# Turnings of x, context and maxima move into the ring of four working banks; their bank becomes a third score bank

## The reference, cut to what matters

```
x = x + layernorm(attention(layernorm(x)))     # 16 heads of 16, block-sparse: blocks of 64 tokens
x = x + layernorm(ffn(layernorm(x)))           # a dense "abel" branch, and 8 experts, the best 2 per token
```

## Time and profile before

| what | value |
|---|---|
| median of 3 runs (lowest to highest) | 1812.6 us (1811.93 to 1817.06) |
| profiled execution, its own time | 1810.62 us |
| its span, first to last instruction | 1808.8 us |
| PE busy | 1542.5 us, 85% |
| DVE busy | 1236.9 us, 68% |
| ACT busy | 897.1 us, 50% |
| POOL busy | 706.6 us, 39% |
| exponentials (L1006) | 768 of 600 ns |
| row maxima (L1168) | 1024 of 546 ns |
| mean granted TensorE clock | 0.956 of full speed |

### The profile page before, as it was taken

How to read it: one execution, slowest core, us unless ns; L and a number is a source line. 1 busy time by engine, 2 the same in 40 slices (tenths; PEclk the granted TensorE clock), 3 DMA queues, 4 the chain that set the end, 5 groups by cost and what they waited for, 6 DMA issues and landing times. The chain is left out here.

```text
span 1808.8 us, 33541 instructions
## 1 busy us (share of the span) xinstructions
PE 1542.5 (85%) x10381; PEld 1072.0 (59%) x10446; DVE 1236.9 (68%) x3681; ACT 897.1 (50%) x1785; POOL 706.6 (39%) x716
## 2 busy tenths in 40 slices
PE   3989999999998998999999888399999999999600
PEld 2645555555555554555555446288888888888500
DVE  6677787778778777877877744355556655565277
ACT  1146766676676667667666672133333333333234
POOL 0111323433343344244234334135444444445468
PEclk9899999999999999999999998699999999999855
DMA  3333235325424533543443226745656565655387
GB/s 100 117 118 98 86 118 171 116 98 173 140 98 154 166 109 106 170 141 112 137 159 117 90 91 199 236 100 102 147 103 146 103 152 105 141 117 112 36 308 251
DMA packets 184525, 241.49 MB, mean 134 GB/s; under 512 B 23560, under 2 KB 155024, under 8 KB 184272
## 3 DMA queue, kind: packets, MB, share of 16 engines
q1 hardware_dynamic: 157520, 203.58, 35.2%
q0 software_dynamic: 26880, 36.33, 12.1%
HBM read 133.40 MB, written 105.91 MB: 132 GB/s over the span
## 5 line engine op out<-in xcount | busy, mean ns | idle before, releaser
L1006 ACT ACTIVATE pexp<-scT 128x512 f32<-128x512 f32 x768 | 434.9, 600 | 275.5 <-PE scT L784 238.7
L1168 DVE TENSOR_REDUCE mx<-work 128x1 f32<-128x320 f32 (+2 forms) x1024 | 499.9, 546 | 70.4 <-PE work L757 70.4
L1679 POOL DMA_INDIRECT y_rows<-rows_add,row_of x144 | 226.5, 1573 | 294.6 <-DMA y_rows<-rows_add,row_of 207.9
L757 PE MATMUL work<-w 126*128 126x320 bf16 (+4 forms) x1280 | 274.9, 298 | 33.1 <-DVE mx L1168 29.6
L784 PE MATMUL scT<-w 128*128 128x192 bf16 (+3 forms) x1472 | 258.5, 270 | 26.0 <-ACT pexp L1006 20.6
L1711 PE MATMUL h_ps<-inT,w1c 128*128 128x256 f32 x1152 | 262.2, 381 | 2.6 <-DVE inT L1763 2.6
L1724 PE MATMUL o_ps<-w,hT 128*128 x1152 | 260.5, 380 | 0.0
L1654 ACT ACTIVATE rows_add<-rows_out,row_share 128x257 f32<-128x257 f32 x144 | 65.6, 503 | 355.5 <-DVE rows_out L1779 276.5
L1711 PEld LDWEIGHTS h_ps<-inT,w1c 128*128 128x128 f32 x1152 | 220.1, 191 | 33.2 <-issue 3.8
L1724 PEld LDWEIGHTS o_ps<-w,hT 128*128 128x128 f32 x1152 | 213.9, 191 | 25.7
L784 PEld LDWEIGHTS scT<-w 128*128 128x128 bf16 x1536 | 125.1, 97 | 162.3 <-ACT pexp L1006 110.4
(11 more groups left out here) (174 smaller groups left out, 2120.8 us busy)
## 6 DMA issues: line engine op xcount, KB each, us to landing
w<-split_spill SPq DMA_DIRECT2D x384, 128.0 KB, 2.9
split_spill<-split SPq DMA_DIRECT2D x64, 384.0 KB, 3.1
rows_in<-z_rows SPq DMA_DIRECT2D x72, 265.0 KB, 4.8
y_rows<-pre SPq DMA_DIRECT2D x16, 514.0 KB, 5.8
y<-y_rows SPq DMA_DIRECT2D x16, 514.0 KB, 6.7
x_rows<-x SPq DMA_DIRECT2D x16, 512.0 KB, 2.6
abel_rows<-pre SPq DMA_DIRECT2D x16, 512.0 KB, 3.5
abel_in<-abel_rows SPq DMA_DIRECT2D x16, 512.0 KB, 4.6
```

Source lines behind the costliest of these rows:

```text
L757: ins = nc.tensor.matmul(out[:, at:at + hi - lo], tile(qst[par][0:K_SCORE, h, :], t), kst[par][0:K_SCORE, h, lo:hi], start=True, stop=True)
L1006: nc.scalar.activation(pexp[:, (q * GROUP + n) % NPB, :], scT[n % 2][:, :], ACT.Exp, scale=DH ** -0.5).then_inc(s_exp, 1)
L1168: emptied(nc.vector.reduce_max(mx[:, c:c + 1], bank(s, "max", b, h, t)[:, 0:n], AX_X), s, "max", b, h, t)
L1679: pool.indirect_dma_start(kept.y_rows, bass.IndirectOffsetOnAxis(ap=row_of[n][:, r:r + 1], axis=0), rows_add[n % 2][:, r, :], None, comput ...
```

## The change

The bank `turn` becomes a third score bank: unit u uses bank u mod 3 and waits for the exponential of unit u-3. The two turnings of x (`xt`), the four of the context (`ctx`) and the two of the maxima (`turnmax`) become items of the ring, with its waits in place of the semaphores s_xt, s_xnT, s_mt, s_m2, s_turn and s_ctxn. In `order_of` each stands where TensorE issues it. On ScalarE the copies of x come after the first exponential of quads 8 and 10, not after the fourth, and the copy of the late maxima after the third exponential of quad 3. On VectorE the subtraction for the late maxima comes ahead of the last two maxima of quad 3, not behind them.

```diff
-        scT = [ps(f"scT{i}", [P, S]) for i in range(2)]
+        scT = [ps(f"scT{i}", [P, S]) for i in range(3)]
         pv = ps("pv", [P, S])
-        turn = ps("turn", [P, S])
...
             for m in range(4):
                 if here(s, 0):
                     seq.append(("project", m))
+                if here(s, 2) and m % 2:
+                    seq.append(("ctx", m // 2))
                 if here(s, 1):
                     maxima(s - 1, late("proj", m))
             if here(s, 3):
                 seq.extend(("z", k) for k in range(KC))
             for q in range(QUADS):
+                if q in TURN_XN and s + 1 < B:
+                    seq.append(("xt", TURN_XN.index(q)))
                 for n in range(GROUP):
                     if here(s, 0) and q < V_QUADS and n == 1:
                         seq.append(("value", q))
+                    if here(s, 2) and q < 2 and n == 2:
+                        seq.append(("ctx", q + 2))
+                    if here(s, 1) and q == LATE_TURN_AT and n == 2:
+                        seq.append(("turnmax", 1))
                     if here(s, 0):
                         maxima(s, fill(q, n))
                         if q == QUADS - 1:
+                            if n == 3:
+                                seq.append(("turnmax", 0))
                             maxima(s, late("end", n))
...
             def turn_xn(b, k):
-                if k == 0:
-                    wait(pe, s_ctxn, (b - 2) * NTOK)
-                    wait(pe, s_m2[1], b - 1)
-                wait(pe, s_xnT, b * KC + k)
+                out = use(b - 1, "xt", k)
...
             def turn_max(b, part):
                 reduced(pe, b, part)
-                if part:
-                    pe.wait_ge(s_m2[0], b + 1)
-                    wait(pe, s_ctxn, b * NTOK)
-                else:
-                    wait(pe, s_ctxn, (b - 1) * NTOK)
-                    pe.wait_ge(s_xnT, min(b + 2, B) * KC)
+                out = use(b + part, "turnmax", part)
...
-                wait(pe, s_exp, u - 1)
+                wait(pe, s_exp, u - 2)
                 for t, at, lo, hi in CHUNKS[c]:
-                    ins = nc.tensor.matmul(scT[n % 2][:, at:at + hi - lo],
+                    ins = nc.tensor.matmul(scT[u % 3][:, at:at + hi - lo],
...
             def turn_ctx(b, j):
                 if j == 0:
                     pe.wait_ge(s_ctxT, (b + 1) * NG)
-                    pe.wait_ge(s_xnT, min(b + 3, B) * KC)
-                    pe.wait_ge(s_m2[0], min(b + 2, B))
-                    pe.wait_ge(s_m2[1], b + 1)
-                wait(pe, s_ctxn, b * NTOK + j)
+                out = use(b + 2, "ctx", j)
...
# ScalarE, step
                         if attend:
                             exps(s - 1, q, n)
+                        if q in TURN_XN and n == 0 and s + 1 < B:
+                            evac_xnT(s + 1, TURN_XN.index(q))
+                        if attend and q == LATE_TURN_AT and n == 2:
+                            first_max(s - 1, 1)
...
-                    if attend and q == LATE_TURN_AT:
-                        first_max(s - 1, 1)
...
-                    if q in TURN_XN and (not isinstance(s, int) or s + 1 < B):
-                        evac_xnT(s + 1, TURN_XN.index(q))
...
# VectorE, step
                     if proj:
                         for n in range(1, GROUP):
+                            if n == 3 and attend and q == LATE_TURN_AT:
+                                second_max(s - 1, 1)
                             for h, t in fill(q, n):
                                 maximum(s, s, h, t)
...
-                    if attend and q == LATE_TURN_AT:
+                    if attend and not proj and q == LATE_TURN_AT:
                         second_max(s - 1, 1)
```

More of the change, by code:

```diff
@@ L437, in order_of @@
             if s < 0:
-                return [("series", n, i) for n in range(SERIES_FIRST) for i in range(NROT)]
+                return [("series", n, i) for n in range(SERIES_FIRST) for i in range(NROT)] \
+                    + [("xt", k) for k in range(KC)]
             seq = []
@@ L568, in put_maxima @@
             def put_maxima(par, b, part):
-                sp.wait_ge(s_m2[part], b + 1)
+                freed(sp, b + part, "turnmax", part)
                 heads = slice(EARLY, HEADS) if part else slice(0, EARLY)
@@ L713, in turn_xn @@
             def turn_xn(b, k):
-                if k == 0:
-                    wait(pe, s_ctxn, (b - 2) * NTOK)
-                    wait(pe, s_m2[1], b - 1)
-                wait(pe, s_xnT, b * KC + k)
+                out = use(b - 1, "xt", k)
                 for j in range(NTOK):
                     pe.wait_ge(s_xn, b * NTOK + j + 1)
-                    ins = nc.tensor.transpose(turn[:, j * P:(j + 1) * P], xn[:, j, k * P:(k + 1) * P],
+                    ins = nc.tensor.transpose(out[:, j * P:(j + 1) * P], xn[:, j, k * P:(k + 1) * P],
                                               ident_sb[:, :])
-                ins.then_inc(s_xt, 1)
+                filled(ins, b - 1, "xt", k)
             def project(b, m):
                 if m == 0:
-                    pe.wait_ge(s_xnT, (b + 1) * KC)
+                    for k in range(KC):
+                        freed(pe, b - 1, "xt", k)
                 col = (m % 2) * D + (m // 2) * P
@@ L765, in turn_max @@
                 reduced(pe, b, part)
-                if part:
-                    pe.wait_ge(s_m2[0], b + 1)
-                    wait(pe, s_ctxn, b * NTOK)
-                else:
-                    wait(pe, s_ctxn, (b - 1) * NTOK)
-                    pe.wait_ge(s_xnT, min(b + 2, B) * KC)
+                out = use(b + part, "turnmax", part)
                 plain(pe)
                 some = mx[:, NT * EARLY:] if part else mx[:, 0:NT * EARLY]
-                nc.tensor.transpose(turn[0:some.shape[1], 0:P], some, ident_sb[:, :]).then_inc(s_mt[part], 1)
+                filled(nc.tensor.transpose(out[0:some.shape[1], 0:P], some, ident_sb[:, :]),
+                       b + part, "turnmax", part)
             def score_unit(b, par, q, n):
@@ L964, in evac_xnT @@
             def evac_xnT(b, k):
-                act.wait_ge(s_xt, b * KC + k + 1)
-                nc.scalar.copy(xnT[:, k, :], turn[:, :]).then_inc(s_xnT, 1)
+                full(act, b - 1, "xt", k)
+                emptied(nc.scalar.copy(xnT[:, k, :], bank(b - 1, "xt", k)[:, :]), b - 1, "xt", k)
             def first_part(b, m):
@@ L980, in first_max @@
             def first_max(b, part):
-                act.wait_ge(s_mt[part], b + 1)
+                full(act, b + part, "turnmax", part)
                 wait(act, s_mrow[part], b * N_MAX * 16)
-                nc.scalar.copy(mrow[part][:, 0, :], turn[0:mrow[part].shape[0], 0:P]).then_inc(s_m1[part], 1)
+                nc.scalar.copy(mrow[part][:, 0, :], bank(b + part, "turnmax", part)[0:mrow[part].shape[0], 0:P])\
+                  .then_inc(s_m1[part], 1)
             def norm_x(b, p, j):
@@ L1010, in evac_ctx @@
                 act.wait_ge(s_pv, b * QUADS + (g + 1) * NCH)
-                if g == 0:
-                    wait(act, s_turn, b * NTOK)
+                if g == 0 and b > 0:
+                    for j in range(NTOK):
+                        full(act, b + 1, "ctx", j)
                 nc.scalar.copy(ctxT[:, g, :], pv[:, :]).then_inc(s_ctxT, 1)
@@ L1172, in second_max @@
                 dve.wait_ge(s_m1[part], b + 1)
-                nc.vector.tensor_tensor(mrow[part][:, 1, :], turn[0:mrow[part].shape[0], 0:P],
-                                        mrow[part][:, 0, :], ALU.subtract).then_inc(s_m2[part], 1)
+                emptied(nc.vector.tensor_tensor(mrow[part][:, 1, :],
+                                                bank(b + part, "turnmax", part)[0:mrow[part].shape[0], 0:P],
+                                                mrow[part][:, 0, :], ALU.subtract), b + part, "turnmax", part)
             def evac_z(s, b, k):
@@ L1184, in finish_a @@
             def finish_a(b, j):
-                dve.wait_ge(s_turn, b * NTOK + j + 1)
-                tv = turn[:, :].rearrange("p (h e) -> p h e", e=32)
+                full(dve, b + 2, "ctx", j)
+                tv = bank(b + 2, "ctx", j)[:, :].rearrange("p (h e) -> p h e", e=32)
                 nc.vector.reciprocal(rden[:, j % 2, :], tv[:, :, DH]).then_inc(s_rden, 1)
@@ L1193, in finish_a @@
                 inv = rden[:, j % 2, :].rearrange("p (h o) -> p h o", o=1).broadcast_to([P, HEADS, DH])
-                nc.vector.tensor_tensor(ctxn[:, j, :].rearrange("p (h d) -> p h d", d=DH),
-                                        tv[:, :, 0:DH], inv, ALU.mult).then_inc(s_ctxn, 1)
-                dve.wait_ge(s_ctxn, b * NTOK + j + 1)
+                emptied(nc.vector.tensor_tensor(ctxn[:, j, :].rearrange("p (h d) -> p h d", d=DH),
+                                                tv[:, :, 0:DH], inv, ALU.mult), b + 2, "ctx", j)
+                freed(dve, b + 2, "ctx", j)
```

12 lines of the change are left out of this document (3 added, 9 removed).

## The result

The changed kernel takes 1841.87 us (median of 4 runs, 1836.99 to 1844.55); the kernel before took 1814.05 us beside it (4 runs, 1811.93 to 1817.06). The ratio is 1.0153, with a 95% interval of [1.0127, 1.0179]. The forecast was 1832, its range 1815 to 1843: the sign and most of the ring's price came out as forecast, but about two fifths of the loss have a cause that the forecast did not hold, a falling clock.

What follows compares the result with a forecast made beforehand. TensorE was taken to bound the front, busy 755.51 of 820.22 us in full steps. Terms -2.1 - 2.0 + 4.9 + 13.7 + 5.0 = +19.5 us on the median 1812.6 gave 1832, range 1815 to 1843.

Steps and rivals of the forecast that it cites:

- The late maxima at quad 3: Quad 3's last maximum must wait for the subtraction that empties the turning: 1.05 us a step, x 13 = +13.7 us.
- rival C: Ring takes turnings with less loss: quad 3's last maximum loses 0.4 us, turnings of x nothing; 1818.5 us, chance 0.14.
- The project phase: Maximum waits for project 0, z 1 for project 3; most returns in quad 1, leaving 0.41 us x 12 = +4.9 us.
- Rival B: Project phase's delay is not taken back: TensorE stays 1.1 us late, not 0.41; 1840 us, chance 0.15.
- The turnings of x: At quads 8 and 10 each waits for a maximum, 0.18 and 0.24 us: 0.42 x 12 = +5.0 us.
- Quads 5 to 7 and 9: Score waits removed there are worth 0: TensorE then waits for the copied context or for VectorE at a maximum.
- Rival A: Score banks were the true limit: 20.6 us of waits come back and no added wait counts; 1792 us, chance 0.07.
- The third bank: In full steps it gains only at quad 11, where nothing but TensorE is late: -0.16 us x 13 = -2.1 us.
- The one-offs outside the full steps: Of 8.0 us of score waits outside the full steps, a quarter is saved: -2.0 us, bounds 0 and -8.0.

Runs made afterwards that it cites:

- e3: Kernel before, own turning bank kept; only the last maximum of quad 3 waits for the late maxima's subtraction, with copy and subtraction placed as changed: 1834.29 us, ratio 1.0118.
- e2: Changed kernel, but a score unit again waits for the exponential two units before, so the third bank gives no slack: 1849.07 us, ratio 1.0209.
- e4: Changed kernel with the two turnings of x at quads 9 and 11 instead of 8 and 10: 1829.83 us, ratio 1.0091.
- e8: Kernel before, own turning bank kept, with x turned at quads 9 and 11 and copied after the first exponential there: 1804.94 us, ratio 0.9956.
- e1: Changed kernel with the turning of the late maxima moved from quad 3 to the end of quad 4: 1836.10 us, ratio 1.0125.
- e7: Changed kernel with the late maxima turned ahead of quad 3's first maximum and subtracted first by VectorE: 1827.51 us, ratio 1.0077.
- e5: Changed kernel with late maxima turned sooner, x turned at quads 9 and 11, and the project phase's second maximum behind project 2: 1805.73 us, ratio 0.9969.

## Why the prediction was right in sign and 10 us short

By the profiled executions, +19.5 was forecast and +33.9 came, 14.4 more. Its terms, one by one:

- **The late maxima at quad 3: right.** 1.05 a step forecast; in step 6 TensorE is 0.43 late entering quad 3 and 1.47 late after it, 1.04 (lateness here is the start of the same matmul, counted from the step's start, against the kernel before); e3 gives the same 1.04 alone. It is the largest single term, with the releaser that was named, and rival C, which had 0.4, is out. Only the sentence that nothing is taken back before quad 7 was wrong: by the rotation's turning in quad 4 the lateness is 1.34, 0.13 less.
- **The project phase: right.** 0.41 forecast, 0.43 late when it leaves quad 1. The mechanism is the one given: z 1 waits 0.55, TensorE is about 1.1 late at z, and quad 1 gives the rest back, where the second abel item's wait is gone. Rival B (nothing given back) is out. Some of the third bank's gain is in this number: without its slack (e2) quad 1 ends another 0.14 later.
- **The turnings of x: right in size.** 0.42 forecast for the two; the even step shows 0.10 to 0.16 for the first and 0.23 to 0.29 for the second. That moving them could fill a wait instead of causing one was seen by e4 and e8 only.
- **Quads 5 to 7 and 9: right, worth nothing.** The context's wait and the maximum's wait took up what the score units lost. (The prediction counts three score waits in the even step; step 6 has four, 0.34, 0.58, 0.39 and 0.16, but its values hold, as quads 5 to 7 were taken together.) Rival A falls with this. The sentence of the Trainium skill (Perfetto Trace Analysis, "Matmul Optimizations") that spoke for A isn't borne out for this change as a whole: all eight banks are in steady use, and the kernel is 1.5% slower. The third score bank by itself does gain, as the next point has it.
- **The third bank: mis-sized.** -0.16 a step was read from the row of quad 11; in step 6 TensorE got back 0.34 there, and e2 gives 0.47 for the bank in all. The idle time in a row is less than the wait, since it counts from the recorded end of the matmul before, which overlaps the start of the next: before, the two score units of quad 11 started 0.56 apart (458.69 and 459.25 in step 6) with 0.16 shown as idle; now 0.22. The same shows at 415.12, where the idle time is 0.59 and the maximum starts 0.75 later than in the step before the change.
- **The one-offs outside the full steps: wrong in sign.** -2.0 was forecast; the steps 0 to 2 took 4.4 more (the first full step starts at 215.39, not 210.98). In steps 1 and 2 the scores did come sooner, by 1.8 and 1.6 us from the step's start, but the first maximum of quad 3 then waits for the stacked q and k, which a DMA brings (3.23 us at 119.91, where the kernel before waited 1.48; 1.89 at 178.68, where it did not wait), and nothing of it is kept. The clock falls behind both waits (granted 0.58 and 0.57 of full speed in the 4 us from 120.0 and from 178.5), and in these stretches TensorE loses 1.4 and 1.6 us against the kernel before: 3.0 of the 4.4 are two more falls.
- **The missing term: the granted clock.** The failed step is the assumption, never written out as a step, that a pause costs its own length. Here 1.5 us of pause at quad 3 (0.77 + 0.73) were followed by a stretch at the lower level in six of the twelve steps, and the 1.48 at quad 9 in a seventh: 11.3 us in all. That the pause brings falls is shown by e3, which adds only the wait, with its two reorderings, to a kernel whose full steps have none.

Together: 11.3 (falls) + 6.4 (one-offs: 4.4 instead of -2.0) - 2.6 (steps 3 to 14 without falls: 17.6 instead of 20.2, of which quad 11 makes -2.2 and quad 4 -1.6, the rest +1.2) - 0.7 (what comes after step 14: 0.6 instead of 1.3, not taken apart) = 14.4. With the two of steps 1 and 2 the falls make 14.3 of it; that the other errors cancel to 0.1 is luck. It is luck too that the median, 1841.87, lies within the range, by 1 us: its upper end was put at 1843 to hold rival B, which did not come about, and the forecast's own bounds, given as 1824 to 1839 (4 and 5 us added make 1823 to 1841), lie below it. By the medians the miss is 9.9 us (1841.87 against 1832), since the profiled execution of the changed kernel was its longest run and that of the kernel before was shorter than its median. Its runs spread over 7.6 us; that of 1836.99 us had a mean granted clock of 0.953, those of 1844.5 us 0.947 and 0.950. With 1.6 us a fall the spread would be a handful of falls more or less; that is argued from the mean clock and not shown step by step.

## What to carry to other kernels

A resource that served rare items out of order hides their waits; put them into a ring that is emptied in order, and each inherits the wait of the item n places before it. Price that at the busiest place of the emptying engine, not at the mean. Before sharing a bank, look for TensorE work that waits for nobody and put it ahead of a place where TensorE waits: that alone was worth as much a step (0.46) as the third bank (0.47), and has no such price. And when a change makes pauses of TensorE longer, look at the granted clock step by step: here a pause of 1.5 us with a fall behind it cost about twice its length.

## What the runs showed of the hardware that was not expected

In a stream in which TensorE is busy about 90% of each step, one or two pauses of 1.5 to 1.8 us together were in many steps followed by a drop of the clock from 2.4 to 1.2 GHz for a stretch of some microseconds (0.57 granted from 571.10 to 575.10; 0.50 from 568.60 to 571.60 in e3), at 1.5 to 1.6 us each. What stood ahead of falls: 0.77 + 0.73 us (after, quad 3), 0.42 + 1.33 (e3, quad 3), 1.19 + 0.29 (e1 and e7, quad 9). What stood in full steps without any: 0.42 + 0.29 and 0.93 + 0.29 (before), 0.56 + 0.29 and 0.76 + 0.29 (e5). This sorts the kernels and not the single steps: the longer pauses stand in steps without a fall too, and in step 1 the kernel before waited 1.48 us for a DMA (119.50) with no fall behind it. The Trainium skill (TensorE: Matmul & The Clock Gate, "A second HAM failure mode: psum-queue depth-cycling") tells of a kernel whose clock swings between the two levels because TensorE pauses briefly and often while it goes round the PSUM banks; the traces here agree in that waits for banks, as listed above, came ahead of the falls, but there is one fall in a step at most.

Open: why a pause of the same rows brings a fall in some steps and none in others. In the changed kernel the waits at quads 3 and 9 are the same to 0.01 us in steps 3 to 7, without falls, as in steps 8 to 14, with falls, but for step 11 (0.94 at quad 3); step 15, with 0.96 + 0.74 there, has no fall. And e7 fell in steps 4, 7, 9, 11 and 13 alone. These rows do not tell such steps apart, and no run was made for it.
